# ACT copies q and k of each even head pair into SBUF whole; DVE makes their high and low parts from there

## The chip, the cores and the metric

The kernel runs on one core of one Trainium2 chip. The metric is device time in microseconds. Engines are named as in the profile: PE is TensorE (PEld its weight loads), DVE is VectorE, ACT is ScalarE, POOL is GpSimd, SP is SyncE.

## What is computed

The input x has 32 batches of 256 tokens with 128 features. Six residual layers follow each other. The last but one of them, a causal softmax attention with 16 heads of 64, takes most of the time:

```python
q = jnp.einsum('qdh,bcd->bhcq', Q, x) * sq
k = jnp.einsum('qdh,bcd->bhcq', K, x) * sq
v = jnp.einsum('vdh,bcd->bhcv', V, x) * sv
att = jnp.einsum('bhcq,bhCq->bhcC', q, k) / d_query
att = jnp.where(causal, att, -jnp.inf)
p = jax.nn.softmax(att, axis=-1)
y = jnp.einsum('bhcC,bhCv->bhcv', p, v)
z = jnp.einsum('dvh,bhcv->bcd', W, y) * (math.sqrt(d_embed / d_value) / num_heads)
```

Before it stand a tanh layer, a linear attention, a second tanh layer and a spectral layer (a circulant matrix), behind it a second spectral layer. Each works on the layer norm of x and adds to x.

## The kernel before

All of x stays in SBUF. The first four layers run over 16 groups of 512 tokens (`phases`); this takes roughly the first fifth of the span. The softmax attention and the last spectral layer then run over the 32 batches, and in each batch over 8 **turns** p = 0 to 7, one for each pair of heads (`batch`, written once for each engine). Pair n = 8b + p; j = p % 2 picks one of two buffers. Two turns, an even and an odd one, make a double turn, four double turns a batch. The order on each engine is the order of the code; every dependence between engines is a semaphore wait written by hand. Line numbers are those of the kernel before.

In turn p:
- PE computes q and k of pair n+2 (`qk_product`, L1033 to L1035, six matmuls into the one PSUM bank BANK_QK), then one piece of other work: values of this or the next batch (`values`, L1068 to L1070, in turns 0, 1, 6, 7), transposes of the next batch's x and of the spectral layer (turn 2), or a third of the output projection of the batch before (`project_out`, L1088, turns 3 to 5). Then it transposes the probabilities of pair n-1 (`probs_transpose`, L1062). In odd turns the scores of pairs n+1 and n+2 follow (`scores`, L1048), and the products of probabilities and values of pairs n-2 and n-1 (`products`, L1079).
- Since fp32r matmuls alone are not exact enough, q and k are split: ACT rounds the bank to a high part (`qk_high`, L744), and DVE subtracts it from the bank for the low part (`qk_low`, L505). The scores use high times high, high times low and low times high.
- DVE takes the reciprocal of the row sums of pair n (`inv_sum`, L527), makes the low part of pair n+2, and copies the larger part of the transposed probabilities of pair n-1 to SBUF (`probs_T`, L534). In odd turns it then masks the scores of two pairs and takes their row maxima (`mask_scores`, L519). In turn 0 it also normalises z for the spectral layer (`z_norm`, L563), in turn 2 it makes the low part of the next batch's x (`x_low`, L499), in turn 6 it takes statistics of z (`z_stats`).
- ACT takes the exponentials (`exp_head`, L759) and copies out y (`y_out`, L785), values (`values_out`, L776) and the rest of the transposed probabilities (`probs_T`, L768).
- POOL scales the probabilities of pair n in SBUF by the reciprocals, with two instructions (`scale_probs`, L325 and L327), and makes the reciprocal standard deviations (in turn 6 those of z, L338 and L340).

Waits that matter here: before `qk_product` of pair n+2 PE waits until the low parts of all pairs up to n+1 are made (`qklo_ready`), since the bank is then free. In turn 3 PE waits for `xlo_ready` before the projection, since both use BANK_X. `probs_transpose` waits for `pTa_ready`, the copy of the pair before by DVE.

Of the kernel before, what the change touches and what calls it, by code (L numbers as in the profile page):

```python
# [14 lines left out]
P = 128  # L15
# [96 lines left out]
def build(nc, x, Wq, bq, Wd, bd, Wu, bu, Wo, bo, W1, W2, W3, ffn_bias, Q, K, V, W, w_re, w_im, fft_bias, dft, out):  # L112
    ctx = ExitStack()
    with ctx:
        def sb(name, shape, dt=F32):
            return ctx.enter_context(nc.sbuf_tensor(name, shape, dt))

        def sem(name):
            return ctx.enter_context(nc.semaphore(name))
# [49 lines left out]
        y0 = sb("y0", [P, GT, P]); yT0 = sb("yT0", [P, GW])  # L169

        x_hi = sb("x_hi", [P, 2, T], F32R); x_lo = sb("x_lo", [P, 2, T], F32R)
        qk_hi = sb("qk_hi", [P, 2, 2, T], F32R); qk_lo = sb("qk_lo", [P, 2, 2, T], F32R)
        neg_max = sb("neg_max", [P, 2, 4]); rsum = sb("rsum", [P, 2, 4]); rinv = sb("rinv", [P, 2, 4])
        pr = sb("pr", [P, 3, 2, 3, P])
# [19 lines left out]
        q_done = sem("q_done"); kv_done = sem("kv_done"); ek_ready = sem("ek_ready"); eq_ready = sem("eq_ready"); v0_ready = sem("v0_ready"); phi_ready = sem("phi_ready")  # L194
        ctx_done = sem("ctx_done"); cbd_ready = sem("cbd_ready"); nd_done = sem("nd_done")
        den_ready = sem("den_ready"); zr_ready = sem("zr_ready"); y0_ready = sem("y0_ready"); y0t_done = sem("y0t_done"); yT0_ready = sem("yT0_ready")
        qk_done = sem("qk_done"); qkhi_ready = sem("qkhi_ready"); qklo_ready = sem("qklo_ready")
        s_done = sem("s_done"); max_ready = sem("max_ready"); exp_ready = sem("exp_ready")
        rinv_ready = sem("rinv_ready"); pn_ready = sem("pn_ready"); pt_done = sem("pt_done")
        pTa_ready = sem("pTa_ready"); pTb_ready = sem("pTb_ready")  # L200
# [157 lines left out]
        def _(dve):  # L358
# [139 lines left out]
                dve.wait_ge(xhi_ready, count(b + 1))  # L498
                nc.vector.tensor_tensor(x_lo[:, j, :], ps[:, BANK_X, 0:T], x_hi[:, j, :].bitcast(F32), ALU.subtract).then_inc(xlo_ready, 1)  # L499

            def qk_low(n, j):
                dve.wait_ge(qkhi_ready, count(n + 1))
                if above_0(2 * n - 2):
                    dve.wait_ge(s_done, count(2 * n - 2))
                nc.vector.tensor_tensor(qk_lo[:, j].rearrange("p s k -> p (s k)"), ps[:, BANK_QK, :],  # L505
                                        qk_hi[:, j].rearrange("p s k -> p (s k)").bitcast(F32), ALU.subtract).then_inc(qklo_ready, 1)

            def mask_scores(n, j):
# [78 lines left out]
            x_low(0, 0)  # L587
            v_low()
            ln_soft_norm(1, 1)
            qk_low(0, 0)  # L590
            qk_low(1, 1)
            mask_scores(0, 0)
            mask_scores(1, 1)
# [1 line left out]
            def batch(b, jb, first=False, last=False):  # L595
                for p in range(PAIRS):
                    n, j = b * PAIRS + p, p % 2
                    if p == LN_TURN + 3 and has_batch(b + 2):
                        ln_soft_norm(b + 2, jb)
                    inv_sum(n, j)  # L600
                    if p == LN_TURN and has_batch(b + 2):
                        ln_soft_stats(b + 2, jb)
                    if p == Z_TURN and not first:
                        z_stats(b - 1)
                    if not (last and p >= PAIRS - 2):
                        qk_low(n + 2, j)
                    if p == 0 and above_0(b - 1):
                        z_norm(b - 2)
                    if p == X_TURN and not last:
                        x_low(b + 1, 1 - jb)  # L610
                    if p == W_TURN + 2 and not first:
                        add_z(b - 1)
                        if above_0(b - 1):
                            add_spectral(b - 2, b)
                    if not (first and p == 0):
                        probs_T(n - 1, 1 - j)
                    if p % 2 == 1 and not (last and p == PAIRS - 1):
                        mask_scores(n + 1, 0)
                        mask_scores(n + 2, 1)
# [12 lines left out]
        def _(act):  # L632
# [106 lines left out]

            def qk_high(n, j):  # L740
                act.wait_ge(qk_done, count(n + 1))
                if above_0(2 * n - 2):
                    act.wait_ge(s_done, count(2 * n - 2))
                nc.scalar.copy(qk_hi[:, j].rearrange("p s k -> p (s k)"), ps[:, BANK_QK, :]).then_inc(qkhi_ready, 1)  # L744

            def exp_head(n, j, h, buf):

# [100 lines left out]
        def _(pe):  # L848
# [270 lines left out]
            values(0, 0, 0)  # L1119
            pe.wait_ge(su_ev, 7)  # L1120
            values(0, 0, 1, FIRST_V_BANKS[1])
            pe.wait_ge(qklo_ready, 1)
            qk_product(1, 1, 0, 1)
            scores(0, 0, 0)
            scores(1, 0, 1)
# [1 line left out]
            def batch(b, jb, first=False, last=False):  # L1127
                for p in range(PAIRS):
                    n, j = b * PAIRS + p, p % 2
                    if not (last and p >= PAIRS - 2):  # L1130
                        pe.wait_ge(qklo_ready, count(n + 2))
                        qk_product(n + 2, (p + 2) % PAIRS, jb if p + 2 < PAIRS else 1 - jb, j)

                    if p < 2:
                        pe.wait_ge(v_ready, count(4 * b + (p + 2)))
                        values(b, jb, p + 2)
                    if p == X_TURN:
                        pe.wait_ge(v_ready, count(4 * (b + 1)))
                        if not last:
                            x_transpose(b + 1, 1 - jb)  # L1140
                        if above_0(b - 1):
                            spectral_transpose(b - 2)
                    if p == W_TURN and not first:
                        if not last:
                            pe.wait_ge(xlo_ready, count(b + 2))
                        if above_0(b - 1):
                            pe.wait_ge(z_xT_ready, count(b - 1))
                    if W_TURN <= p < W_TURN + len(W_STEPS) and not first:
                        project_out(b - 1, 1 - jb, W_STEPS[p - W_TURN])
                    if p == W_TURN + len(W_STEPS) - 1 and above_0(b - 1):  # L1150
                        spectral_product(b - 2)
                    if p == V_TURN and not last:
                        pe.wait_ge(xlo_ready, count(b + 2))
                        if not first:
                            pe.wait_ge(x_ready, count(b + SOFT))
                        if above_0(b - 1):
                            pe.wait_ge(out_ready, count(b - 1))
                    if p > V_TURN and not last:
                        pe.wait_ge(v_ready, count(4 * (b + 1) + (p - V_TURN)))
                    if p >= V_TURN and not last:  # L1160
                        values(b + 1, 1 - jb, p - V_TURN)

                    if not (first and p == 0):
                        probs_transpose(n - 1, 1 - j, pr_of(p - 1), b * (PAIRS // 2) + p // 2)
                    if p % 2 == 1:
                        if not (last and p == PAIRS - 1):
                            scores(n + 1, jb if p + 1 < PAIRS else 1 - jb, 0)
                            scores(n + 2, jb if p + 2 < PAIRS else 1 - jb, 1)
                        pe.wait_ge(pTb_ready, count(n))
                        if p > 1:  # L1170
                            products(n - 2, p - 2, jb, 1, 0)
                        elif not first:
                            products(n - 2, PAIRS - 1, 1 - jb, 1, 0)
                        products(n - 1, p - 1, jb, 0, 1)
# [42 lines left out]
```

## Time and profile before

| | |
|---|---|
| median of 3 runs | 1324.78 us (1324.59 to 1326.14) |
| profiled execution | 1325.28 us |
| its span in the trace | 1323.5 us |
| PE busy | 1247.6 us, 94% of the span |
| PEld busy | 1067.1 us, 81% |
| DVE busy | 1025.3 us, 77% |
| ACT busy | 934.0 us, 71% |
| POOL busy | 589.4 us, 45% |

One execution was profiled; the busy time of an engine is the time in which at least one of its instructions ran. PE's ends are modelled, and matmuls overlap, so starts are the safer numbers.

### The profile page before, as it was taken

To read this page: it belongs to the slowest core of one execution; us is meant where nothing else is said; L and a number is where in the kernel's file an instruction comes from. 1 tells how busy PE (TensorE), PEld (TensorE's weight loads), DVE (VectorE), ACT (ScalarE), POOL (GpSimd) and SP (SyncE) were. 2 spreads that over 40 slices of the span, in tenths; PEclk is the share of its full clock that TensorE was granted. 3 is DMA by queue.
4 is the path that set the end of the run, shared out by engine and by line. 5 is a ranking of instruction groups with operands and counts; after the bars stand their busy time and mean duration, and the time that the engine had idled before them with its cause. 6 is when DMAs were issued, how large, how long until landed. Compare 5 with 4: busy or idle time off the path is not lost.

```text
span 1323.5 us, 38816 instructions
## 1 busy us (share of the span) xinstructions
PE 1247.6 (94%) x11323; PEld 1067.1 (81%) x11331; DVE 1025.3 (77%) x4813; ACT 934.0 (71%) x3265; POOL 589.4 (45%) x913
## 2 busy tenths in 40 slices
PE   5799987899999999999999999999999999999997
PEld 4688866778888888888888888888888888888885
DVE  6977779877777777777777777777777777777774
ACT  4745357577777777777777777777777777777773
POOL 4812137534444444444444444444444444444442
PEclk9999989999999999999999999999999999999999
DMA  8000000000000000000000000000000000000000
GB/s 212 1 1 0 1 1 0 1 2 1 2 9 0 8 0 8 0 8 0 8 0 8 0 8 0 8 0 8 0 8 0 8 0 8 0 8 0 9 1 17
DMA packets 14301, 11.80 MB, mean 9 GB/s; under 512 B 709, under 2 KB 12522, under 8 KB 14058
## 3 DMA queue, kind: packets, MB, share of 16 engines
q1 hardware_dynamic: 14240, 11.19, 3.2%
q8 instruction: 23, 0.38, 0.1%
q14 instruction: 28, 0.23, 0.1%
q10 hardware_dynamic: 10, 0.00, 0.0%
HBM read 7.00 MB, written 4.19 MB: 8 GB/s over the span
## 4 chain that ended last, share of the span: by engine, by line
PE 57%; ACT 17%; issue 11%; DVE 10%; POOL 2%; DMA 1%; SPq 1%; ACTq 0%; DVEq 0%; POOLq 0%
PE ps L1048 9%; ACT pr L759 9%; PE ps L1079 9%; PE ps L1088 9%; PE ps L1062 6%; PE ps L1033 5%; ACT qk_hi L744 4%; PE ps L1035 3%; PE ps L1034 3%; DVE qk_lo L505 3%; DVE pT L534 2%; PE ps L962 2%; PE ps L920 1%; ACT pT L768 1%; PE ps L980 1%
## 5 line engine op out<-in xcount | busy, mean ns | idle before, releaser
L759 ACT ACTIVATE pr<-ps,neg_max 128x128 f32<-128x128 f32 (+1 forms) x1024 | 424.6, 430 | 165.2 <-DVE neg_max L519 165.2
L325 POOL TENSOR_TENSOR pr<-pr,rinv 128x256 f32<-128x256 f32 x256 | 156.9, 613 | 572.9 <-DVE rinv L527 572.9
L519 DVE CUSTOM_DVE_ANT_0 ps<-ps,mask 128x128 f32<-128x128 f32 (+1 forms) x1024 | 329.2, 389 | 8.0 <-issue 6.2
L327 POOL TENSOR_TENSOR pr<-pr,rinv 128x512 f32<-128x512 f32 x256 | 266.3, 1040 | 0.0
L505 DVE TENSOR_TENSOR qk_lo<-ps,qk_hi 128x512 fp32r<-128x512 f32 x256 | 176.9, 691 | 114.6 <-ACT qk_hi L744 114.1
L759 ACT ACTIVATION_READ_ACCUMULATOR pr<-ps,neg_max 128x1 f32 x1024 | 218.1, 213 | 0.0
L1062 PE MATMUL ps<-ident,pr 128*128 128x128 f32 x1536 | 209.9, 272 | 1.9 <-POOL pr L327 0.9
L534 DVE COPY pT<-ps 128x512 f32<-128x512 f32 x256 | 175.2, 685 | 29.8 <-PE ps L1062 26.0
L1062 PEld LDWEIGHTS ps<-ident,pr 128*128 128x128 f32 x1536 | 179.3, 140 | 20.4 <-issue 2.2
L1079 PE MATMUL ps<-pT,space 128*64 128x256 f32 (+1 forms) x2048 | 194.9, 332 | 0.7 <-ACT pT L768 0.5
L1033 PE MATMUL ps<-x_hi,wqk_hi 128*128 128x256 f32 x512 | 169.8, 332 | 18.2 <-DVE qk_lo L505 14.0
L1079 PEld LDWEIGHTS ps<-pT,space 128*64 128x64 f32 x2048 | 126.8, 136 | 55.1 <-ACT pT L768 0.7
L768 ACT COPY pT<-ps 128x256 f32<-128x256 f32 x256 | 102.3, 400 | 83.0 <-PE ps L1062 82.9
L744 ACT CAST qk_hi<-ps 128x512 fp32r<-128x512 f32 x256 | 154.5, 604 | 7.9 <-PE ps L1035 1.3
L1048 PE MATMUL ps<-qk_hi 64*128 64x128 f32 (+1 forms) x1024 | 156.2, 301 | 0.5 <-DVE qk_lo L505 0.5
L1033 PEld LDWEIGHTS ps<-x_hi,wqk_hi 128*128 128x128 f32 x512 | 96.2, 188 | 63.4 <-DVE qk_lo L505 41.2
L1034 PE MATMUL ps<-x_lo,wqk_hi 128*128 128x256 f32 x512 | 144.4, 282 | 0.0
L1035 PE MATMUL ps<-x_hi,wqk_lo 128*128 128x256 f32 x512 | 144.3, 282 | 0.0
L1048 PE MATMUL ps<-qk_lo,qk_hi 64*128 64x128 f32 (+1 forms) x1024 | 142.7, 275 | 0.0
L1048 PE MATMUL ps<-qk_hi,qk_lo 64*128 64x128 f32 (+1 forms) x1024 | 142.1, 274 | 0.0
L519 DVE DVE_READ_ACCUMULATOR2_ANT neg_max<- 128x1 f32 x1024 | 141.8, 138 | 0.0
L1088 PE MATMUL ps<-wz,space 128*128 128x128 f32 x1024 | 129.7, 275 | 0.6 <-ACT space L793 0.6
(168 smaller groups left out, 2356.7 us busy)
## 6 DMA issues: line engine op xcount, KB each, us to landing
out<-x_all SPq DMA_DIRECT2D x16, 256.0 KB, 2.3
x_all<-L_attn_x SPq DMA_DIRECT2D x1, 768.0 KB, 6.3
x_all<-L_attn_x SPq DMA_DIRECT2D x1, 512.0 KB, 3.9
space<-L_attn_Q SPq DMA_DIRECT2D x1, 512.0 KB, 15.4
space<-L_attn_K SPq DMA_DIRECT2D x1, 512.0 KB, 9.6
space<-L_attn_V SPq DMA_DIRECT2D x1, 512.0 KB, 11.6
space<-L_attn_W SPq DMA_DIRECT2D x1, 512.0 KB, 12.0
dft_s<-dft SPq DMA_DIRECT2D x1, 192.0 KB, 2.9
```

What stands on the lines that cost most here:

```text
L327: nc.gpsimd.tensor_tensor(pr[:, buf, :, 1:3, :].rearrange("p h b k -> p h (b k)"), pr[:, buf, :, 1:3, :].rearrange("p h b k -> p h (b k)") ...
L505: nc.vector.tensor_tensor(qk_lo[:, j].rearrange("p s k -> p (s k)"), ps[:, BANK_QK, :], qk_hi[:, j].rearrange("p s k -> p (s k)").bitcast( ...
L519: last = nc.vector.tensor_tensor_reduce(o, o, mask[:, T - w:T], -1.0, -MASKED, ALU.add, ALU.min, neg_max[:, j, 2 * h + qt:2 * h + qt + 1])
L534: nc.vector.tensor_copy(pT[:, j].rearrange("p h b q -> p (h b q)")[:, 0:512], ps[:, BANK_T, :]).then_inc(pTa_ready, 1)
L744: nc.scalar.copy(qk_hi[:, j].rearrange("p s k -> p (s k)"), ps[:, BANK_QK, :]).then_inc(qkhi_ready, 1)
L759: last = nc.scalar.activation(dst, ps[:, BANK_S + 2 * j + h, qt * P:qt * P + w], ACT.Exp, bias=neg_max[:, j, at:at + 1], scale=-1.0, accum ...
L1033: mm(o, wqk_hi[:, s, of_pair], x_hi[:, jb, :], start=True, stop=False, skip_group_check=True)
L1034: mm(o, wqk_hi[:, s, of_pair], x_lo[:, jb, :], start=False, stop=False, skip_group_check=True)
L1048: last = mm(ps[:, BANK_S + 2 * j + h, qt * P:qt * P + w], q[of_head, j, 0, qt * P:(qt + 1) * P], key[of_head, j, 1, 0:w], start=(k == 0), ...
L1062: last = tr(to, pr[:, buf, k // 3, k % 3, :], ident[:])
L1079: last = mm(ps[k * DV:(k + 1) * DV, BANK_Y, half * T + kt * P:(half + 1) * T], vv[:, jb, kt, h * DV:(h + 1) * DV], pT[:, j, k, 0:2, :] if ...
L1088: last = mm(ps[:, BANK_X, t * D:(t + 1) * D], yT[:, j, p, t * P:(t + 1) * P], wz[:, p, :], start=(p == 0), stop=(p == PAIRS - 1), skip_gro ...
```

## The change

In an even turn (j = 0) ACT copies the whole bank, unrounded, to a new SBUF tile `qk_raw` and signals `qk_out`. DVE then makes the high part from `qk_raw` by a cast (its new `qk_high`), and the low part by subtracting that high part from `qk_raw`. In odd turns (j = 1) all is as before: ACT rounds the bank to the high part, DVE subtracts it from the bank; only the semaphore that ACT raises is now `qk_out` too. In odd turns PE's `qk_product` (whose bank holds an even pair till then) waits for `qk_out` in place of `qklo_ready`; in even turns it waits for `qklo_ready` as before. ACT waits, before it fills `qk_raw`, for the low part of the even pair before. In turn 0 `z_norm` now stands between the two DVE steps.

```diff
+        qk_raw = sb("qk_raw", [P, 2 * T])
...
-            def qk_low(n, j):
-                dve.wait_ge(qkhi_ready, count(n + 1))
+            def qk_high(n, j):
+
+                dve.wait_ge(qk_out, count(n + 1))
                 if above_0(2 * n - 2):
                     dve.wait_ge(s_done, count(2 * n - 2))
-                nc.vector.tensor_tensor(qk_lo[:, j].rearrange("p s k -> p (s k)"), ps[:, BANK_QK, :],
+                nc.vector.tensor_copy(qk_hi[:, j].rearrange("p s k -> p (s k)"), qk_raw[:]).then_inc(qkhi_ready, 1)
+
+            def qk_low(n, j, evens=0):
+                if j == 0:
+                    dve.wait_ge(qkhi_ready, count(evens))
+                    whole = qk_raw[:]
+                else:
+                    dve.wait_ge(qk_out, count(n + 1))
+                    whole = ps[:, BANK_QK, :]
+                if above_0(2 * n - 2):
+                    dve.wait_ge(s_done, count(2 * n - 2))
+                nc.vector.tensor_tensor(qk_lo[:, j].rearrange("p s k -> p (s k)"), whole,
                                         qk_hi[:, j].rearrange("p s k -> p (s k)").bitcast(F32), ALU.subtract).then_inc(qklo_ready, 1)
...
-                    if not (last and p >= PAIRS - 2):
-                        qk_low(n + 2, j)
+                    if p % 2 == 0 and not (last and p >= PAIRS - 2):
+                        qk_high(n + 2, j)
                     if p == 0 and above_0(b - 1):
                         z_norm(b - 2)
+                    if not (last and p >= PAIRS - 2):
+                        qk_low(n + 2, j, b * (PAIRS // 2) + (p // 2 + 2))
...
             def qk_high(n, j):
                 act.wait_ge(qk_done, count(n + 1))
-                if above_0(2 * n - 2):
-                    act.wait_ge(s_done, count(2 * n - 2))
-                nc.scalar.copy(qk_hi[:, j].rearrange("p s k -> p (s k)"), ps[:, BANK_QK, :]).then_inc(qkhi_ready, 1)
+                if j == 0:
+                    if above_0(n - 1):
+                        act.wait_ge(qklo_ready, count(n - 1))
+                    nc.scalar.copy(qk_raw[:], ps[:, BANK_QK, :]).then_inc(qk_out, 1)
+                else:
+                    if above_0(2 * n - 2):
+                        act.wait_ge(s_done, count(2 * n - 2))
+                    nc.scalar.copy(qk_hi[:, j].rearrange("p s k -> p (s k)"), ps[:, BANK_QK, :]).then_inc(qk_out, 1)
...
-                        pe.wait_ge(qklo_ready, count(n + 2))
+                        pe.wait_ge(qk_out if p % 2 else qklo_ready, count(n + 2))
                         qk_product(n + 2, (p + 2) % PAIRS, jb if p + 2 < PAIRS else 1 - jb, j)
```

The steps on DVE in turn 2, from the reciprocal of this turn to that of turn 3; before:

```order
L527 RECIPROCAL rinv<-rsum 128x4 [waits pn_ready,exp_ready]
L502 REGISTER_ALU
L505 TENSOR_TENSOR qk_lo<-ps,qk_hi 128x512 [waits s_done,qkhi_ready]
L498 REGISTER_ALU
L499 TENSOR_TENSOR x_lo<-ps,x_hi 128x256 [waits xhi_ready]
L531 REGISTER_ALU
L534 COPY pT<-ps 128x512 [waits pv_done,pt_done]
L527 RECIPROCAL rinv<-rsum 128x4 [waits pn_ready,exp_ready]
```

and with the change (L507 is the new cast, L518 the low part, L500 the low part of x, L547 the copy of transposed probabilities, L540 the reciprocal):

```order
L540 RECIPROCAL rinv<-rsum 128x4 [waits pn_ready,exp_ready]
L504 REGISTER_ALU
L507 CAST qk_hi<-qk_raw 128x512 [waits s_done,qk_out]
L511 REGISTER_ALU
L518 TENSOR_TENSOR qk_lo<-qk_raw,qk_hi 128x512 [waits s_done,qkhi_ready]
L499 REGISTER_ALU
L500 TENSOR_TENSOR x_lo<-ps,x_hi 128x256 [waits xhi_ready]
L544 REGISTER_ALU
L547 COPY pT<-ps 128x512 [waits pv_done,pt_done]
L540 RECIPROCAL rinv<-rsum 128x4 [waits pn_ready,exp_ready]
```

The cast and a low part that reads SBUF twice stand where one low part stood, ahead of `x_lo` and `pT`.

The steps on DVE in turn 0, where z is normalised; before:

```order
L527 RECIPROCAL rinv<-rsum 128x4 [waits pn_ready,exp_ready]
L502 REGISTER_ALU
L505 TENSOR_TENSOR qk_lo<-ps,qk_hi 128x512 [waits s_done,qkhi_ready]
L563 TENSOR_SCALAR z_xn<-x_all,z_mv,z_rstd 128x128 [waits z_tr_done,z_rstd_ready]
L563 TENSOR_SCALAR z_xn<-x_all,z_mv,z_rstd 128x128
L534 COPY pT<-ps 128x512 [waits pv_done,pt_done]
L527 RECIPROCAL rinv<-rsum 128x4 [waits pn_ready,exp_ready]
```

and with the change (L576 is the normalising of z):

```order
L540 RECIPROCAL rinv<-rsum 128x4 [waits pn_ready,exp_ready]
L504 REGISTER_ALU
L507 CAST qk_hi<-qk_raw 128x512 [waits s_done,qk_out]
L576 TENSOR_SCALAR z_xn<-x_all,z_mv,z_rstd 128x128 [waits z_tr_done,z_rstd_ready]
L576 TENSOR_SCALAR z_xn<-x_all,z_mv,z_rstd 128x128
L511 REGISTER_ALU
L518 TENSOR_TENSOR qk_lo<-qk_raw,qk_hi 128x512 [waits s_done,qkhi_ready]
L547 COPY pT<-ps 128x512 [waits pv_done,pt_done]
L540 RECIPROCAL rinv<-rsum 128x4 [waits pn_ready,exp_ready]
```

The cast has come ahead of the two instructions on z, and the low part behind them; `pT` still comes last.

PE at the end of an even turn and the start of an odd one (L1062 transposes probabilities, L1033 to L1035 make q and k); before:

```order
L1062 MATMUL ps<-ident,pr 128x128 [waits pTa_ready,pn_ready]
L1062 MATMUL ps<-ident,pr 128x128 x3
L1062 MATMUL ps<-ident,pr 128x128 [waits y_ready,pTb_ready]
L1062 MATMUL ps<-ident,pr 128x128
L1033 MATMUL ps<-x_hi,wqk_hi 128x256 [waits qklo_ready]
L1034 MATMUL ps<-x_lo,wqk_hi 128x256
L1035 MATMUL ps<-x_hi,wqk_lo 128x256
L1033 MATMUL ps<-x_hi,wqk_hi 128x256
```

and with the change (L1083 and L1054 to L1056 are the same lines):

```order
L1083 MATMUL ps<-ident,pr 128x128 [waits pTa_ready,pn_ready]
L1083 MATMUL ps<-ident,pr 128x128 x3
L1083 MATMUL ps<-ident,pr 128x128 [waits y_ready,pTb_ready]
L1083 MATMUL ps<-ident,pr 128x128
L1054 MATMUL ps<-x_hi,wqk_hi 128x256 [waits qk_out]
L1055 MATMUL ps<-x_lo,wqk_hi 128x256
L1056 MATMUL ps<-x_hi,wqk_lo 128x256
L1054 MATMUL ps<-x_hi,wqk_hi 128x256
```

The order is the same; the first matmul of q and k waits for `qk_out`.

## Rows read from the trace of the kernel before

**Rows 1.** Who waited for whom, whole span: us in total, times, longest us
```profile
PEld ps L1033 <- DVE qk_lo L505: 41.2, 96, 1.5
```

**Rows 2.** Timeline of PE, turns 2 to 5: start us, us, engine, line
```profile
799.70 0.82 PE L1062 MATMUL ps<-ident,pr 128*128 128x128 f32 x6
...
800.83 0.38 PE L1033 MATMUL ps<-x_hi,wqk_hi 128*128 128x256 f32 x1 [0.31 <-DVE qk_lo L505]
...
801.64 1.50 PE L1088 MATMUL ps<-wz,space 128*128 128x128 f32 x12
...
802.98 0.82 PE L1062 MATMUL ps<-ident,pr 128*128 128x128 f32 x6
...
808.91 0.82 PE L1062 MATMUL ps<-ident,pr 128*128 128x128 f32 x6
...
809.48 0.37 PE L1033 MATMUL ps<-x_hi,wqk_hi 128*128 128x256 f32 x1
...
811.73 0.82 PE L1062 MATMUL ps<-ident,pr 128*128 128x128 f32 x6
```

**Rows 3.** Timeline of PE, turns 6 and 7
```profile
817.01 0.82 PE L1062 MATMUL ps<-ident,pr 128*128 128x128 f32 x6
...
817.88 0.39 PE L1033 MATMUL ps<-x_hi,wqk_hi 128*128 128x256 f32 x1
...
819.40 0.82 PE L1062 MATMUL ps<-ident,pr 128*128 128x128 f32 x6
```

**Rows 4.** Timeline of PE, turns 0 and 1 of the next batch
```profile
824.71 0.82 PE L1062 MATMUL ps<-ident,pr 128*128 128x128 f32 x6
...
825.57 0.39 PE L1033 MATMUL ps<-x_hi,wqk_hi 128*128 128x256 f32 x1
...
827.08 0.82 PE L1062 MATMUL ps<-ident,pr 128*128 128x128 f32 x6
```

**Rows 5.** Timeline of ACT, the high parts of turns 2, 6 and 0
```profile
799.47 0.59 ACT L744 CAST qk_hi<-ps 128x512 fp32r<-128x512 f32 x1
...
816.52 0.59 ACT L744 CAST qk_hi<-ps 128x512 fp32r<-128x512 f32 x1
...
824.20 0.59 ACT L744 CAST qk_hi<-ps 128x512 fp32r<-128x512 f32 x1
```

**Rows 6.** Timeline of DVE, turns 2 and 0
```profile
800.69 0.41 DVE L499 TENSOR_TENSOR x_lo<-ps,x_hi 128x256 fp32r<-128x256 f32 x1
...
801.02 0.68 DVE L534 COPY pT<-ps 128x512 f32<-128x512 f32 x1
...
824.82 0.69 DVE L505 TENSOR_TENSOR qk_lo<-ps,qk_hi 128x512 fp32r<-128x512 f32 x1 [0.92 <-ACT qk_hi L744]
...
825.43 0.60 DVE L563 TENSOR_SCALAR z_xn<-x_all,z_mv,z_rstd 128x128 f32 x2
...
825.94 0.69 DVE L534 COPY pT<-ps 128x512 f32<-128x512 f32 x1
```

**Rows 7.** Timeline of POOL, turns 2, 4, 6 and 0
```profile
799.83 1.04 POOL L327 TENSOR_TENSOR pr<-pr,rinv 128x512 f32<-128x512 f32 x1
...
808.08 1.04 POOL L327 TENSOR_TENSOR pr<-pr,rinv 128x512 f32<-128x512 f32 x1
...
816.82 1.04 POOL L327 TENSOR_TENSOR pr<-pr,rinv 128x512 f32<-128x512 f32 x1
...
818.09 0.76 POOL L340 TENSOR_TENSOR z_rstd<-z_veps,half_neg 128x2 f32<-128x2 f32 x1
...
824.55 1.04 POOL L327 TENSOR_TENSOR pr<-pr,rinv 128x512 f32<-128x512 f32 x1
```

**Rows 8.** Timeline of DVE and POOL in the first batch that normalises z
```profile
338.45 1.43 DVE L563 TENSOR_SCALAR z_xn<-x_all,z_mv,z_rstd 128x128 f32 x2
338.50 1.04 POOL L327 TENSOR_TENSOR pr<-pr,rinv 128x512 f32<-128x512 f32 x1
```

**Rows 9.** Timeline of DVE, setup: a cast in SBUF, 512 elements a partition
```profile
12.70 0.42 DVE L373 CAST bias_bf<-rest 1x512 bf16<-1x512 f32 x1
```

More of the change, by code:

```diff
@@ L196, in build @@
         den_ready = sem("den_ready"); zr_ready = sem("zr_ready"); y0_ready = sem("y0_ready"); y0t_done = sem("y0t_done"); yT0_ready = sem("yT0_ready")
-        qk_done = sem("qk_done"); qkhi_ready = sem("qkhi_ready"); qklo_ready = sem("qklo_ready")
+        qk_done = sem("qk_done"); qk_out = sem("qk_out"); qkhi_ready = sem("qkhi_ready"); qklo_ready = sem("qklo_ready")
         s_done = sem("s_done"); max_ready = sem("max_ready"); exp_ready = sem("exp_ready")
@@ L589, in _ @@
             ln_soft_norm(1, 1)
-            qk_low(0, 0)
+            qk_high(0, 0)
+            qk_low(0, 0, 1)
             qk_low(1, 1)
@@ L1121, in _ @@
             values(0, 0, 1, FIRST_V_BANKS[1])
-            pe.wait_ge(qklo_ready, 1)
+            pe.wait_ge(qk_out, 1)
             qk_product(1, 1, 0, 1)
```

## The prediction

> **What bounds the kernel now.** I read the list of waits first, then the timeline of each engine over one batch of the softmax stage. PE is the engine that is hardly ever idle there, and the one wait of any size on its side is this: the first weight load of q and k waits for DVE's low part [rows 1]. The timeline says where. In even turns q and k follow the products without a wait. In odd turns they follow the transposes of probabilities, and the least distance from the start of those to the start of q and k is 0.57 us, in turns 4 and 5 (808.91 to 809.48) [rows 2]. Against it, turns 2 and 3 take 1.13 (0.56 lost), turns 6 and 7 take 0.87 (0.30 lost) and turns 0 and 1 take 0.86 (0.29 lost) [rows 2 to 4]. That is 1.15 us a batch, some 36 us in all. It is what the change aims at, and the most that it can return.
>
> The second thing to see is how DVE stands. Behind the low part of an even turn it still has, in order: z's normalising (turn 0) or x's low part (turn 2), then the copy of transposed probabilities. PE waits for x's low part before the projection of turn 3 and for the copy before the transposes of the odd turn. Those two deadlines have little slack, as the sums below show.
>
> **Part by part.** *ACT*: its instruction keeps its shape and place, so I leave it at 0.59 us; `qk_raw` is done at 800.06 in turn 2, 817.11 in turn 6 and 824.79 in turn 0 [rows 5]. Its new wait is for a low part made a double turn earlier: nothing. The wait for the scores that it drops ended nothing.
>
> *PE*: it needs only ACT's copy in odd turns. With 0.57 us behind the transposes, q and k could start at 800.27, 817.58 and 825.28; ACT is done before each. So the old wait goes entirely. What is late next is DVE.
>
> *The cast on DVE*: 128 times, new work. The nearest row is a cast in SBUF with 512 elements a partition, 0.42 us [rows 9]; as an upper end I take the low part's own 0.69 [rows 6], one element at a time. I take 0.42, as the row is of the same operation and width.
>
> But it will not start freely. ACT's copy ends inside POOL's long scaling in all these turns: POOL's instruction runs 799.83 to 800.87 in turn 2, 816.82 to 817.86 in turn 6, 824.55 to 825.59 in turn 0 [rows 7]. The trace has one clear case of a DVE instruction that reads and writes only SBUF meeting it: two normalising instructions took 1.43 us beside a POOL scaling that began 0.05 later [rows 8], where the same two take 0.60 otherwise [rows 6]. The DVE pair ended 0.34 us behind POOL's end, so it stood still while POOL ran. So I let the cast wait for POOL's end. How much is left of it then? The blocked pair had spent 0.26 of its 0.60 before it was stopped; if the cast does so too, 0.42 less 0.26 leaves 0.16; if nothing of it is done, 0.42 is left. I take the middle, 0.28. The cast ends at 801.15, 818.14 and 825.87.
>
> The Trainium skill (SBUF — State Buffer, Who interferes with whom) speaks against the change here: a DVE copy or cast that uses both port pairs and a GpSimd instruction shut each other out for the whole instruction, whoever starts first; the trace agrees [rows 8]. By that rule the sum is the forecast; without it, the first rival.
>
> *The low part* now reads two SBUF tiles; I keep 0.69, and 0.61 from its start to the next start [rows 6]. From an end to a waiting start I use 0.03 on DVE (ACT's 824.79 to 824.82) and 0.06 from DVE to PE (825.51 to 825.57) [rows 4 to 6].
>
> *Turns 2 and 3*: low part 801.18, x's low part 801.79, ended 802.20 (0.41 long), projection at 802.26 instead of 801.64: **0.62 later** [rows 2, 6]. The transposes follow it by 1.34, at 803.60. The copy of probabilities starts 0.33 behind x's low part and ends by 802.81, in time.
>
> *Turns 0 and 1*: z's two instructions from 825.87, 0.51 to the next start, low part 826.38, copy of probabilities 826.99 to 827.68, transposes at 827.74 instead of 827.08: **0.66 later** [rows 4, 6].
>
> *Turns 6 and 7*: low part 818.17, copy 818.78 to 819.47, transposes at 819.53 instead of 819.40: **0.13 later** [rows 3].
>
> *Turns 4 and 5*: POOL ends at 809.12, the cast at 809.40, the low part starts at 809.43, the copy ends at 810.73; PE wants it at 811.73 [rows 2, 7]. Nothing lost, nothing gained.
>
> Each loss moves PE's scores, and with them masks, exponentials and POOL's scaling, by as much, so the next double turn meets the same pattern. Nothing gives it back: PE is last in each. Turn 0 pays in 30 batches (z is first normalised in the third), turn 3 in 30 (not the first, not the last), turn 7 in 31: 30 x 1.28 + 31 x 0.13 = 42.4 us. The profiled execution took 1325.28 us, which gives 1367.7; the median shown is 0.5 lower, so **1367 us**, 3.2% slower. The bounds of the cast's remainder (0.16 and 0.42) move about 91 places by 0.13 each, 12 us to either side.
>
> **Rivals.**
> 1. *POOL doesn't hold the cast* (0.42 from ACT's end). Turns 2 and 3: cast to 800.51, low part 800.54, x's 801.15 to 801.56, projection 801.62, no change. Turns 0 and 1: transposes at 827.11, +0.03. Turns 6 and 7: the copy ends at 818.89, PE comes at its own pace at 819.10, 0.30 earlier. Net 9 us faster: **1316**. For it: only pairs with pointer scalars were seen held. It decides if less than about 0.1 us of the overlap with POOL is lost. The Trainium skill (VectorE: DVE Perf Modes, the errata's cycle table) prices such a cast at 58 + 512/2 cycles of 0.96 GHz, 0.33 us, an estimate under the row's 0.42; by it this case would be 1311, and the forecast stays, as POOL's end sets it.
> 2. *The cast to the rounded type runs one element at a time*, 0.69 us, and isn't held: turn 3 +0.26, turn 1 +0.30, turn 7 -0.18, net +11: **1336**. For it: no row has this output type from DVE out of SBUF.
> 3. *DVE's lateness is absorbed* and the whole wait returns: -36, **1289**. Against it: the two deadlines above.
> 4. *The low part is held too.* In turn 6 POOL works on z's deviations till 818.85 (818.09 and 0.76) [rows 7]; if the low part can't start before, turn 7 loses 0.68 more in 31 batches: **1388**. The Trainium skill (same page and section as above) has a DVE instruction with two SBUF inputs contend with a GpSimd one that reads SBUF. The rows don't show it for so small a POOL tile.
>
> That the change does not do what it says I exclude: the order of instructions shows the cast and the new wait.
>
> **Chances.** Forecast 0.58, rival 1 0.13, rival 2 0.14, rival 3 0.03, rival 4 0.08, and 0.04 for gain and loss that cancel. About 0.2% (2.6 us) is what a measurement of this kernel can tell from no change. Faster: 0.13 + 0.03 = 0.16; same: 0.04; slower: 0.80. The range takes in the forecast with its bounds, rival 2 and rival 4: 1328 to 1390; rivals 1 and 3 stay outside.
>
> **What would show it.** Right: the cast's time in the trace is near 1 us in turns 0, 2 and 6, and ends some 0.3 us behind POOL's scaling; PE's wait on the low part is gone in odd turns, and in its place PE waits for the low part of x before the projection (turn 3) and for the copy of probabilities (turn 1). Wrong: a cast of 0.4 us beside POOL (rival 1) or 0.7 (rival 2), or POOL's scaling growing in place of the cast, which would mean that DVE gets in first.

## The result

The changed kernel takes 1417.26 us (median of four), the kernel before 1324.68 us. One of the four ran in a slow state (1746.91 us, granted clock 0.655), and without it the median is 1414.36 us and the ratio 1.068, with a 95% interval of 1.065 to 1.071. The profiled execution took 1412.18 us. Slower was forecast, but 1367 us with a range up to 1390; the loss is twice what the sum gave.

The page of the changed kernel (span; busy time of each engine; the queue that brings instructions):

```profile
span 1410.4 us, 39177 instructions
PE 1276.2 (90%) x11331; PEld 1081.5 (77%) x11331; DVE 1144.6 (81%) x4941; ACT 942.7 (67%) x3265; POOL 627.5 (44%) x913
q14 instruction: 94, 0.76, 0.2%
```

and that queue on the page of the kernel before:

```profile
q14 instruction: 28, 0.23, 0.1%
```

The work has grown on DVE (1025.3 to 1144.6 us busy). PE is busy 29 us longer (1247.6 to 1276.2) with the same matmuls, and the clock granted to it is 0.976 on average where it was 0.993. The line that the forecast did not look at is the last: 66 more transfers of instructions.

The waits of the changed kernel (us in total, times, longest), where [rows 1] showed the wait for the low part:

```profile
PEld ps L1083 <- issue: 80.1, 68, 3.0
PE ps L1083 <- DVE pT L547: 53.0, 65, 2.6
PEld ps L1109 <- DVE x_lo L500: 31.2, 30, 1.5
```

The wait of [rows 1] is gone from the list. In its place stand the two waits that the forecast named: for the copy of transposed probabilities (L547) and for x's low part (L500). But single waits are up to 3.0 us long, and no step of the forecast makes one longer than a microsecond.

DVE and POOL in turns 0 and 2 of one batch of the changed kernel, against [rows 6] and [rows 7]:

```profile
801.30 1.02 DVE L507 CAST qk_hi<-qk_raw 128x512 fp32r<-128x512 f32 x1 [0.96 <-ACT qk_raw L761]
802.24 0.59 DVE L576 TENSOR_SCALAR z_xn<-x_all,z_mv,z_rstd 128x128 f32 x2
...
809.61 1.01 DVE L507 CAST qk_hi<-qk_raw 128x512 fp32r<-128x512 f32 x1 [0.96 <-ACT qk_raw L761]
```

```profile
800.99 1.04 POOL L328 TENSOR_TENSOR pr<-pr,rinv 128x512 f32<-128x512 f32 x1
...
809.30 1.04 POOL L328 TENSOR_TENSOR pr<-pr,rinv 128x512 f32<-128x512 f32 x1
```

The casts end at 802.32 and 810.62, 0.29 and 0.28 us behind POOL's 802.03 and 810.34. That is the forecast of 0.28 to the hundredth. So the excess lies elsewhere. The trace shows it once in two batches, at the jump back of DVE's loop (whose body is two batches; a run through it is called a round here). DVE, then the one ACT row that matters, and PE's next weight load:

```profile
833.71 0.46 DVE L532 CUSTOM_DVE_ANT_0 ps<-ps,mask 128x256 f32<-128x256 f32 x1
834.09 0.14 DVE L532 DVE_READ_ACCUMULATOR2_ANT neg_max<- 128x1 f32 x1
836.72 0.18 DVE L540 RECIPROCAL rinv<-rsum 128x4 f32<-128x4 f32 x1 [2.49 <-ACT pr L780]
...
833.96 0.60 ACT L806 COPY space<-ps 128x512 f32<-128x512 f32 x1
...
840.18 0.64 PEld L1083 LDWEIGHTS ps<-ident,pr 128*128 128x128 f32 x6 [3.02 <-issue]
```

In the kernel before the same place reads:

```profile
855.72 0.46 DVE L519 CUSTOM_DVE_ANT_0 ps<-ps,mask 128x256 f32<-128x256 f32 x1
856.10 0.14 DVE L519 DVE_READ_ACCUMULATOR2_ANT neg_max<- 128x1 f32 x1
856.22 0.18 DVE L527 RECIPROCAL rinv<-rsum 128x4 f32<-128x4 f32 x1
```

DVE does nothing for 2.49 us. The view puts it down to ACT's exponentials, but ACT had gone on to its next copy at 833.96. A wait whose named releaser was long done is a wait for something else. Counted in the trace from one jump back to the next, DVE's loop body has 367 recorded instructions before and 391 after.

### The profile page after: what moved, and what is told of

Read it like the earlier page. It is cut to its first block, busy times and chain, and to the rows that moved or that the text cites. A ratio compares the mean times of both kernels' runs of the same rounds, so it can differ in the third digit from the quotient of the medians.

```text
span 1410.4 us, 39177 instructions
## 1 busy us (share of the span) xinstructions
PE 1276.2 (90%) x11331; PEld 1081.5 (77%) x11331; DVE 1144.6 (81%) x4941; ACT 942.7 (67%) x3265; POOL 627.5 (44%) x913
## 4 chain that ended last, share of the span: by engine, by line
PE 31%; issue 31%; POOL 19%; DVE 12%; ACT 5%; DMA 1%; POOLq 1%; SPq 1%; DVEq 0%; ACTq 0%
POOL pr L328 9%; POOL pr L326 6%; PE ps L1069 5%; PE ps L1109 4%; PE ps L1100 4%; PE ps L1083 4%; ACT pr L780 2%; POOL z_rstd L341 2%; DVE pT L547 2%; PE ps L941 2%; PE ps L983 2%; PE ps L963 2%; DVE qk_hi L507 1%; DVE qk_lo L518 1%; POOL rstd L311 1%
## 5 line engine op out<-in xcount | busy, mean ns | idle before, releaser
L1083 PE MATMUL ps<-ident,pr 128*128 128x128 f32 x1536 | 214.1, 276 | 54.9 <-DVE pT L547 53.0
L1083 PEld LDWEIGHTS ps<-ident,pr 128*128 128x128 f32 x1536 | 176.2, 142 | 89.8 <-issue 80.1
L1100 PE MATMUL ps<-pT,space 128*64 128x256 f32 (+1 forms) x2048 | 203.4, 342 | 0.7 <-ACT pT L789 0.5
L547 DVE COPY pT<-ps 128x512 f32<-128x512 f32 x256 | 175.0, 683 | 33.5 <-PE ps L1083 33.5
L789 ACT COPY pT<-ps 128x256 f32<-128x256 f32 x256 | 98.2, 384 | 141.5 <-PE ps L1083 140.0
L507 DVE CAST qk_hi<-qk_raw 128x512 fp32r<-128x512 f32 x128 | 116.3, 908 | 79.6 <-ACT qk_raw L761 79.3
L1100 PEld LDWEIGHTS ps<-pT,space 128*64 128x64 f32 x2048 | 131.4, 141 | 59.4 <-issue 7.7
L1054 PE MATMUL ps<-x_hi,wqk_hi 128*128 128x256 f32 x512 | 168.5, 329 | 0.3 <-ACT qk_raw L761 0.3
L1069 PE MATMUL ps<-qk_hi 64*128 64x128 f32 (+1 forms) x1024 | 160.1, 309 | 0.5 <-DVE qk_lo L518 0.5
L1069 PE MATMUL ps<-qk_lo,qk_hi 64*128 64x128 f32 (+1 forms) x1024 | 146.8, 283 | 0.0
L1109 PEld LDWEIGHTS ps<-wz,space 128*128 128x128 f32 x1024 | 122.1, 191 | 32.0 <-DVE x_lo L500 31.2
L1069 PE MATMUL ps<-qk_hi,qk_lo 64*128 64x128 f32 (+1 forms) x1024 | 146.5, 282 | 0.0
L1056 PE MATMUL ps<-x_hi,wqk_lo 128*128 128x256 f32 x512 | 144.6, 282 | 0.0
L1069 PEld LDWEIGHTS ps<-qk_hi 64*128 64x128 f32 x1024 | 100.9, 193 | 22.8 <-issue 21.6
```

The costliest lines, as they stand in the source:

```text
L547: nc.vector.tensor_copy(pT[:, j].rearrange("p h b q -> p (h b q)")[:, 0:512], ps[:, BANK_T, :]).then_inc(pTa_ready, 1)
L1054: mm(o, wqk_hi[:, s, of_pair], x_hi[:, jb, :], start=True, stop=False, skip_group_check=True)
L1056: last = mm(o, wqk_lo[:, s, of_pair], x_hi[:, jb, :], start=False, stop=True, skip_group_check=True)
L1069: last = mm(ps[:, BANK_S + 2 * j + h, qt * P:qt * P + w], q[of_head, j, 0, qt * P:(qt + 1) * P], key[of_head, j, 1, 0:w], start=(k == 0), ...
L1083: last = tr(to, pr[:, buf, k // 3, k % 3, :], ident[:])
L1100: last = mm(ps[k * DV:(k + 1) * DV, BANK_Y, half * T + kt * P:(half + 1) * T], vv[:, jb, kt, h * DV:(h + 1) * DV], pT[:, j, k, 0:2, :] if ...
```

## The experiments

**pad_before**: the kernel before, with long fulfilled waits added.

```diff
             def probs_T(n, j):
 
+                dve.wait_ge(v_ready, 1)
+                dve.wait_ge(su_lo, 6)
                 dve.wait_ge(pt_done, count(n + 1))
```

> The kernel before, with two more waits on constants, long fulfilled, ahead of every copy of transposed probabilities on DVE: some 30 short instructions more in the body of DVE's loop, nothing else. Theory A (DVE's loop body has outgrown what stays on the chip, 367 recorded instructions before, 391 after the change, so each jump back stands still some 3 us): the gap at DVE's jump back grows from 0.3 to about 3.4 us in each of 15 rounds, instruction transfers rise from 28 to about 94, and the time from 1325 to about 1370 us. Theory B (the extra loss comes from the port or the order of work and the gap at the jump is a consequence): 1325 to 1328 us and no gap.

Measured: 1324.72 us, ratio 0.9998 (0.9984 to 1.0011), 28 transfers. Of the 32 waits added to the loop body only 16 show as recorded instructions: it has 383. So 383 cost nothing, which speaks neither for nor against size above that.

**slim_after**: the changed kernel with a smaller loop body.

```diff
                     dve.wait_ge(qk_out, count(n + 1))
                     whole = ps[:, BANK_QK, :]
-                if above_0(2 * n - 2):
-                    dve.wait_ge(s_done, count(2 * n - 2))
```

> The changed kernel without the wait for s_done in DVE's low part, which is implied by the waits before it: some 16 short instructions fewer in DVE's loop body (391 to about 375). Theory A: if 375 fits, the gap at the jump back is 0.3 us again and the time falls from 1414 to about 1367 us, the forecast; if it does not fit, nothing changes. Theory B: 1412 to 1418 us.

Measured: 1377.85 us, ratio 1.041 (1.038 to 1.044); 375 instructions, 28 transfers; profiled execution 1373.23 us. Taking away 16 short instructions gives 39 us back between the profiled executions (36.5 between the medians, 1414.36 and 1377.85). What is left is the forecast's own case, and it can be read against its steps. PE, from turn 6 on:

```profile
808.94 0.82 PE L1081 MATMUL ps<-ident,pr 128*128 128x128 f32 x6
...
811.55 0.84 PE L1081 MATMUL ps<-ident,pr 128*128 128x128 f32 x6 [0.21 <-DVE pT L545]
...
816.86 0.81 PE L1081 MATMUL ps<-ident,pr 128*128 128x128 f32 x6
...
819.96 0.85 PE L1081 MATMUL ps<-ident,pr 128*128 128x128 f32 x6 [0.63 <-DVE pT L545]
...
825.01 0.82 PE L1081 MATMUL ps<-ident,pr 128*128 128x128 f32 x6
...
827.51 1.60 PE L1107 MATMUL ps<-wz,space 128*128 128x128 f32 x12 [0.96 <-DVE x_lo L500]
828.95 0.82 PE L1081 MATMUL ps<-ident,pr 128*128 128x128 f32 x6
```

From transposes to transposes: turns 6 to 7 take 2.61 against 2.39 [rows 3], 0 to 1 take 3.10 against 2.37 [rows 4], 2 to 3 take 3.94 against 3.28 [rows 2]: +0.22, +0.73 and +0.66, where 0.13, 0.66 and 0.62 were forecast. Turns 4 to 5 take 2.83 (800.84 to 803.67) against 2.82, the "nothing" of the forecast.

**noscale**: as slim_after, POOL without its scaling in even turns. It leaves out that part of the computation.

```diff
             def scale_probs(n, j, buf):
 
                 pool.wait_ge(rinv_ready, count(n + 1))
+                if j == 0:
+                    nc.gpsimd.tensor_tensor(shift[:, 0, 0:1], half_neg[:, 0:1], minus_1[:, 0:1], ALU.mult).then_inc(pn_ready, 1)
+                    return
```

> As slim_after, and POOL leaves out the scaling of the probabilities of even pairs (one tiny instruction in its place), so nothing of POOL runs beside the cast in even turns. Part of the computation is left out. Port theory: the cast takes 0.42 in place of 1.0 us, the losses in turns 1 and 3 vanish and turn 7 gains 0.3; if the loop fits, 1316 us. Rival (the cast is slow by itself, 1.0 us whatever POOL does): as slim_after, about 1367 us.

Measured: 1325.20 us, ratio 1.0001 (0.9988 to 1.0014). All casts take 0.43 us. Against slim_after that is 53 us less: the whole remaining loss goes with the scaling beside DVE's work. The run takes away all that the scaling does to DVE in even turns; that it is the cast that was held, 1.01 for 0.43 us, is read from the rows above. But it is not the 1316 us of rival 1. PE in turns 6 and 7:

```profile
818.19 0.81 PE L1084 MATMUL ps<-ident,pr 128*128 128x128 f32 x6
818.76 0.37 PE L1055 MATMUL ps<-x_hi,wqk_hi 128*128 128x256 f32 x1
...
820.43 0.82 PE L1084 MATMUL ps<-ident,pr 128*128 128x128 f32 x6
...
824.33 0.39 PE L1055 MATMUL ps<-x_hi,wqk_hi 128*128 128x256 f32 x1
```

The 0.30 us is gained behind the transposes (0.57 to q and k, where [rows 3] had 0.87), but 1.67 in place of 1.52 pass to the next transposes, and 3.90 in place of 3.78 (819.40 to 823.18 before) from there to the next q and k. The gain is given back within the same double turn: the first matmul of the values (819.63) starts just behind ACT's copy of the values before (ended 819.57), and the second pair's scores (822.00) just behind DVE's low part of the odd pair (ended 821.87). Turns 2 to 3 lose 0.09 as well, 3.37 against 3.28, at the wait for x's low part.

**late_split**: as slim_after, DVE's cast and low part of even pairs last in the turn.

```diff
-                    if p % 2 == 0 and not (last and p >= PAIRS - 2):
-                        qk_high(n + 2, j)
+                    if p % 2 == 1 and not (last and p >= PAIRS - 2):
+                        qk_low(n + 2, j)
                     if p == 0 and above_0(b - 1):
                         z_norm(b - 2)
-                    if not (last and p >= PAIRS - 2):
-                        qk_low(n + 2, j, b * (PAIRS // 2) + (p // 2 + 2))
...
                     if not (first and p == 0):
                         probs_T(n - 1, 1 - j)
+                    if p % 2 == 0 and not (last and p >= PAIRS - 2):
+                        qk_high(n + 2, j)
+                        qk_low(n + 2, j, b * (PAIRS // 2) + (p // 2 + 2))
```

> As slim_after, but DVE makes the high and low part of an even pair behind the low part of x and behind the copy of transposed probabilities, since PE needs them only for the scores of the odd turn. Theory (the loss beyond the loop is only that cast and low part stand ahead of two deadlines of PE): the waits for pT and x_lo vanish, PE has no wait in odd turns, all of 1.15 us a batch is gained less some tail in turn 7: 1290 to 1300 us if the loop fits, 45 more if not. Rival (DVE's total load or POOL's ports bind wherever the cast stands): 1350 us or more.

Measured: 1311.83 us, ratio 0.990 (0.987 to 0.993), faster than both kernels but short of 1300. The casts lie behind POOL's scaling and take 0.42 (the middle one of 128). What PE waits for in turn 7 now, PE and DVE:

```profile
812.12 0.50 PE L1088 MATMUL ps<-v_hi,x_hi 128*128 128x512 f32 x1
...
814.35 0.28 PE L1068 MATMUL ps<-qk_hi,qk_lo 64*128 64x256 f32 x2
814.60 0.33 PE L1068 MATMUL ps<-qk_hi 64*128 64x128 f32 x2
...
813.80 0.66 DVE L516 TENSOR_TENSOR qk_lo<-ps,qk_hi 128x512 fp32r<-128x512 f32 x1
```

The second pair's scores start 0.25 us behind the first's last step, and DVE's low part of the odd pair ended at 814.46, just before. The first matmul of the values takes 0.50 where it takes 0.39 without a wait; it waits for ACT's copy of the values before.

**odd_first**: as late_split, with ACT's high part of the odd pair ahead of two exponentials, and DVE's low part ahead of the reciprocal.

```diff
+                    if p % 2 == 1 and not (last and p >= PAIRS - 2):
+                        qk_low(n + 2, j)
                     inv_sum(n, j)
...
                     if not (last and p >= PAIRS - 2):
                         qk_high(n + 2, j)
+                    if p % 2 == 1:
+                        exp_head(n, 1, 1, pr_of(p))
...
-                    if p % 2 == 0:
-                        exp_head(n + 1, 1, 1, pr_of(p + 1))
-                    elif not (last and p == PAIRS - 1):
+                    if p % 2 == 1 and not (last and p == PAIRS - 1):
```

> As late_split, but in odd turns ACT makes the high part of the odd pair before the last two exponentials, and DVE its low part before the reciprocal. Theory (what binds turns 0, 1, 6 and 7 in late_split is ACT's row of work: the low part of the odd pair is ready 0.1 us too late for the scores, and values come 0.15 late): another 0.3 us in each of two double turns a batch, 1290 to 1300 us. Rival (the exponentials then come too late for the masks or the reciprocals): 1312 us or more.

Measured: 1306.21 us, ratio 0.985 (0.983 to 0.987). The fastest here, but a third of what was expected of this step: the odd pair's low part was one of the things that came late, not all of them. The wait for the values remains (the first matmul still takes 0.50 in turn 7), as its order on ACT was left alone.

**late_bank**: as slim_after, PE waits for the low part again in odd turns.

```diff
-                        pe.wait_ge(qk_out if p % 2 else qklo_ready, count(n + 2))
+                        pe.wait_ge(qklo_ready, count(n + 2))
```

> As slim_after, but PE waits in odd turns for the low part again, not for ACT's copy: the cast and the low part that reads SBUF, without what they were meant to buy. By the steps of the forecast q and k of the odd turn would start at 801.93, 810.18, 818.92 and 827.13 in place of 800.83, 809.48, 817.88 and 825.57 of the kernel before: 4.4 us a batch, 1460 us. Rival (the early release buys little): within 15 us of slim_after, 1378.

Measured: 1464.79 us, ratio 1.106 (1.103 to 1.108). So the early release is worth 87 us to slim_after, and the cast and what it delays cost more than that, 140 us against the kernel before.

**pool_waits**: as slim_after, POOL starts behind the cast in even turns.

```diff
                 pool.wait_ge(rinv_ready, count(n + 1))
+                if after_cast is not None:
+                    pool.wait_ge(qkhi_ready, count(after_cast))
```

> As slim_after, but in even turns POOL begins to scale only when the cast is done. If the first to start keeps the other out, the cast takes 0.43 everywhere, and then either z's normalising and the low part, which read two SBUF tiles or use both ports, are held by POOL's scaling (durations of 1 us and more), or POOL's instructions are held by the low part (0.61 grows to 1.2 and more). Time 1345 to 1385 us, so no gain to speak of. Rival (only casts meet POOL): low part 0.69 and POOL 0.61 and 1.04 as before, time about 1330 us.

Measured: 1382.53 us, ratio 1.044 (1.042 to 1.046). All casts take 0.43. DVE, then POOL:

```profile
815.08 1.29 DVE L422 TENSOR_SCALAR xn<-x_all,mv,rstd 128x128 f32 x2
...
821.97 0.89 DVE L576 TENSOR_SCALAR z_xn<-x_all,z_mv,z_rstd 128x128 f32 x2
822.78 1.54 DVE L518 TENSOR_TENSOR qk_lo<-qk_raw,qk_hi 128x512 fp32r<-128x512 f32 x1
...
830.97 0.69 DVE L518 TENSOR_TENSOR qk_lo<-qk_raw,qk_hi 128x512 fp32r<-128x512 f32 x1
```

```profile
822.74 1.03 POOL L330 TENSOR_TENSOR pr<-pr,rinv 128x512 f32<-128x512 f32 x1
...
831.02 1.12 POOL L328 TENSOR_TENSOR pr<-pr,rinv 128x256 f32<-128x256 f32 x1 [4.32 <-DVE qk_hi L509]
```

The low part, both inputs in SBUF, takes 1.54 us where POOL started 0.04 before it; where it started 0.05 ahead of POOL it takes 0.69, and POOL's 0.61 becomes 1.12. The first row, a normalising of x, takes 1.29 in place of 0.59 and started 0.09 behind a scaling (814.99). Each way round, the later one stands still. Moving POOL only moves the loss. (The edit's other half hands the count to `scale_probs` in even turns.)

**pad_more**: as pad_before, with `dve.wait_ge(su_hi, 6)` in addition for every second copy.

> As pad_before, with one more wait on a constant ahead of every second copy: 391 recorded instructions in DVE's loop body, as in the changed kernel, where 383 cost nothing. Theory A (the size of the loop body alone): the gap at each jump back is some 3 us, instruction transfers near 94, time 1365 to 1375 us. Theory B (size is not the cause, but the s_done waits that slim_after dropped, or the cast): 1325 us.

Measured: 1324.23 us, ratio 0.9996 (0.9985 to 1.0007), 28 transfers. Of 40 added waits 17 show as instructions: the body came to 384, not 391, and the run tells only that 384 is free. For a larger body instructions of another kind were needed.

**grow_24** and **grow_18**: the kernel before with one-column memsets of a tile that nothing reads, ahead of the copy of probabilities in each turn, one or two a turn (grow_24's is shown; grow_18 has two in turn 1 alone).

```diff
+                    for k in range({0: 1, 1: 2, 2: 1, 3: 2, 4: 1, 5: 2, 6: 1, 7: 2}[p]):
+                        nc.vector.memset(pad[:, 32 * jb + 4 * p + k:32 * jb + 4 * p + k + 1], 0.0)
                     if not (first and p == 0):
                         probs_T(n - 1, 1 - j)
```

> pad_more came to 384 recorded instructions in DVE's loop body only, and nothing happened. This is the kernel before with 24 one-column memsets of 0.06 us spread over the loop body: 391 recorded instructions, exactly as in the changed kernel, and nothing else changed. Theory A (size of the loop body): the jump back stands still some 3 us in each of 15 rounds, instruction transfers near 94, 1365 to 1380 us. Theory B (the stall belongs to the change itself, not to size): 1325 to 1330 us, since the memsets lie where DVE waits.

> The same with 18 memsets: 385 recorded instructions, one over the 384 that cost nothing in pad_more. If the limit lies right at 384: as grow_24, 1365 to 1380 us. If it is somewhat higher: 1325 to 1330 us.

Measured: grow_24 (391 instructions) 1348.03 us, ratio 1.018 (1.015 to 1.021); grow_18 (385) 1364.59 us, ratio 1.030 (1.027 to 1.033); 93 transfers of instructions in both. Both lose, but grow_24, which was to lose 40 to 55 us, lost 23, and less than grow_18. The memsets themselves (0.059 us each) might have a part in it, so one was taken away:

**grow_17**: as grow_18, with one memset less in every second batch (a body of 384).

```diff
-                    for k in range({0: 1, 1: 2, 2: 1, 3: 1, 4: 1, 5: 1, 6: 1, 7: 1}[p]):
+                    for k in range({0: 1, 1: 2 - jb, 2: 1, 3: 1, 4: 1, 5: 1, 6: 1, 7: 1}[p]):
```

> The kernel before with 17 one-column memsets in DVE's loop body in place of grow_18's 18: a body of 384 recorded instructions, and one memset less in every second batch. If the loss of grow_18 (1364.6 us, 93 transfers of instructions) is the jump back of a body over 384, this run takes 1323 to 1327 us, as pad_more did with 384, and shows 28 transfers. If instead the memsets themselves cost time, by holding DVE between its other work, it loses 17/18 of grow_18's 40 us: 1362 us.

Measured: 1323.34 us, ratio 0.9987 (0.9978 to 0.9997). Its page beside that of grow_18:

```profile
q14 instruction: 28, 0.23, 0.1%
```

```profile
q14 instruction: 93, 0.76, 0.2%
```

Seventeen memsets cost nothing, the eighteenth costs 41 us. The jump back of DVE's loop, the rows of before, slim_after, grow_17, grow_24, grow_18 and the changed kernel in this order (duration min/median/max in ns, first and last start in us):

```profile
L95 DVEq COMPARE_BRANCH  x15: 47/56/69, 334.5 to 1243.8; - x15
```

```profile
L95 DVEq COMPARE_BRANCH  x15: 47/56/69, 337.7 to 1290.2; - x15
```

```profile
L95 DVEq COMPARE_BRANCH  x15: 47/56/69, 333.8 to 1242.1; - x15
```

```profile
L95 DVEq COMPARE_BRANCH  x15: 47/63/69, 335.5 to 1268.7; - x15
```

```profile
L95 DVEq COMPARE_BRANCH  x15: 47/63/69, 333.1 to 1283.2; - x15
```

```profile
L95 DVEq COMPARE_BRANCH  x15: 47/63/80, 337.7 to 1328.8; - x15
```

First to last start, over 14, is the mean length of a round: 64.95, 68.04, 64.88, 66.66, 67.86 and 70.79 us. The changed kernel pays 2.75 us a round over slim_after, 14 x 2.75 = 38.5 us, against 39 between their profiled executions; grow_18 pays 2.98 over grow_17, 41.7 us against the 41.3 between their medians. The first start is the way into the loop and the last leaves it, so 13 jumps back carry this. In grow_18 five transfers of 8 KB on the instruction queue start behind each of these 13 (65 in all, the difference of 93 and 28), the first within a microsecond of the jump; in grow_17 that queue is silent from 381 to 1243 us.

The mean hides two kinds of round. Single rounds of grow_24, of grow_18 (two) and of the changed kernel (three), from jump to jump (window and its length in us; busy time of PE, PEld, DVE, ACT and POOL; granted clock; DMA share and GB/s):

```profile
601.10:667.80 66.70, 64.11 (x620) 54.86 (x618) 51.74 (x269) 49.36 (x182) 29.32 (x40) 1.00 0.02 5
```

```profile
465.70:532.90 67.20, 64.17 (x620) 54.91 (x618) 51.67 (x263) 49.33 (x182) 29.30 (x40) 1.00 0.02 5
601.00:669.30 68.30, 65.51 (x620) 56.10 (x618) 51.73 (x263) 49.32 (x182) 29.30 (x40) 0.98 0.02 4
```

```profile
692.60:762.40 69.80, 64.47 (x622) 54.91 (x620) 58.45 (x255) 49.58 (x183) 31.94 (x40) 1.00 0.02 4
833.10:904.10 71.00, 66.00 (x622) 55.90 (x620) 57.92 (x255) 49.63 (x183) 31.94 (x40) 0.98 0.02 4
475.80:548.10 72.30, 67.58 (x622) 57.27 (x620) 57.95 (x255) 49.66 (x183) 31.93 (x40) 0.95 0.01 4
```

In some rounds the clock granted to PE falls to its lower level (0.50, which is 1.2 GHz), 5 to 9 us behind the jump. In the round at 833.10 PE stands still for 2.61 us up to 840.22, and then runs a stretch at the lower level:

```profile
841.90:845.30 3.40, 3.40 (x26) 2.44 (x24) 2.70 (x21) 1.72 (x8) 0.53 (x1) 0.50 0.00 0
```

grow_24 has no such fall in its loop: its 13 rounds behind a jump take 66.7 to 66.9 us, against 64.87 in grow_17, +1.9 each. grow_18 has two rounds without one (67.2 and 67.4, +2.4) and 11 with 3.4 us at the lower level (68.1 to 68.3, +3.3). The changed kernel, against 67.97 in slim_after, has five without (69.7 to 69.8, +1.8), three with 3.4 us (70.7 to 71.0) and five with 6.8 us (72.0 to 72.6). Its jumps at the full clock thus cost what grow_24's do, 13 x 1.8 = 23 us, and the falls add 16 (the first round, which follows no jump, is 0.7 us shorter than slim_after's).

## Why the prediction was wrong

Slower was right, and so was the mechanism that was summed; the sum was short by one whole term, what a longer loop body costs.

- *The wait of PE for the low part goes*: right. It is gone from the waits, and late_bank shows what it was worth.
- *The cast waits for POOL's end and ends 0.28 us behind*: right (0.28 and 0.29). That it is right to the hundredth is luck: 0.28 was the middle between 0.16 and 0.42, and the 0.16 rested on [rows 8], where 0.26 us of the blocked pair were done though POOL began only 0.05 behind it. noscale, with no scaling beside the cast, takes 53 us off slim_after.
- *Turn 3 +0.62, turn 1 +0.66, turn 7 +0.13, turn 5 nothing*: measured in slim_after +0.66, +0.73, +0.22 and +0.01. The sum of 42 us was mis-sized by some 6: slim_after's profiled execution is 48 above 1325.28 (its median 53 above). PE starts up to 0.15 us behind the copy that it waits for (811.40 to 811.55), where the forecast had 0.06.
- *Rival 1, 1316 us if POOL doesn't hold the cast*: the case was made in noscale, and gave 1325. Its step "PE comes at its own pace" in turns 6 and 7 was wrong: PE gives the 0.30 us back to a copy of values and to the odd pair's low part. And turn 3, which it had on time by 0.02 us, loses 0.09 to x's low part. (Its own terms come to 8.4 us, where it says 9; the 1316 stands.)
- *"The most that it can return"*, 36 us: too much for the same reason. The best order found returns 19 us (odd_first), most of it in turns 2 and 3 (2.86 in place of 3.28 from transposes to transposes); turns 0, 1, 6 and 7 hardly gain.
- *Rival 4, the low part is held too*: the hold is real (1.54 us in pool_waits), but it did not strike where it was priced. In slim_after the low part of turn 6 takes 0.69 us.
- **The step that failed** is "the cast on DVE: 128 times, new work". It was priced by its duration alone. A cast with its waits and its register steps is also some 3 instructions a double turn in the body of DVE's loop: 367 became 391. The runs put the limit between 384 (grow_17 and pad_more, free) and 385 (grow_18, 41 us). Past it, each of the 13 jumps back costs 1.8 to 2.4 us at the full clock, and in 8 of the changed kernel's 13 rounds the clock then falls as well: 23 and 16 us, 39 together. The forecast had neither term. The profile had two things to look at: a loop body of two batches written out, and a queue that brings instructions.

Together: 1325 + 48 (POOL and order) + 39 (loop body, with the clock) = 1412, the profiled execution; the 48 and 39 are differences of profiled executions, and the lengths of rounds give the 39 a second time (38.5). The same 391 instructions cost 23 us in grow_24 and 39 in the changed kernel because of the clock: exactly in the 8 rounds with a fall DVE stands still a second time, for 2.0 to 3.4 us ahead of the cast of turn 2, as PE's slower matmuls bring q and k late. Two things stay open. One is what decides whether the clock falls: PE stands still behind the jump for 1.4 to 1.7 us in grow_24, 1.8 to 2.1 in grow_18 and 2.3 to 2.6 in the changed kernel, but the two rounds of grow_18 without a fall have stops as long (2.05 and 1.88) as those with one. The other is why a jump costs 2.4 us with 385 instructions and 1.8 to 1.9 with 391.

The Trainium skill (Runtime: NRT & Kernel Launch, Instruction fetch mechanics) says that a jump to code that is no longer held on the engine makes it wait for a transfer. The runs agree on the kind of cost: in the 13 rounds behind a jump grow_18 has 65 transfers, grow_17 none. The limit between 384 and 385 recorded instructions and the price are the runs' own. The page's figure of 512 instructions held would have passed both bodies as fitting; the runs decide.

## What to carry to other kernels

Where an engine runs a loop whose body is written out, count its instructions before and after an edit, waits and register steps too, and watch the number of instruction transfers: a single instruction can cost 3% (grow_18 against grow_17). Where such a stop reaches PE, look at the granted clock round by round: part of the price can be PE's clock (16 of 39 us here), and a mean over the loop hides it. When an early release frees a waiting engine, the work that made it wait has a new deadline, later than the old one: move it behind what has an earlier deadline, or the release buys nothing (slim_after 1378, late_split 1312). Copies out of SBUF on DVE and scaling in SBUF on POOL are better placed one behind the other where neither is urgent.

## What the runs showed of the hardware that was not expected

- DVE's loop body of 384 recorded instructions jumps back at no cost; with 385 there are 93 instead of 28 transfers of instructions and a round is 3.0 us longer on average (grow_18 against grow_17). No run shows whether the limit depends on where the body starts.
- The clock of PE can fall to its lower level behind such a stop: 3.4 us in 11 of 13 rounds of grow_18, some 0.9 us longer each; 3.4 or 6.8 us in 8 of 13 of the changed kernel, 1 to 2.8 us longer; never in grow_24's loop.
- Most added waits on constants leave no recorded instruction: of 40 in the loop body 17 did (pad_more).
- A subtraction on DVE with both inputs in SBUF and a multiplication on POOL in SBUF shut each other out in both directions: 1.54 instead of 0.69 us, 1.12 instead of 0.61.
